# Four accumulator groups in every sum of a Runge-Kutta scan, and one matmul moved behind a signal

## The reference

```python
def _derivative(q, p, drive, coupling, bias):
    i_couple = jnp.tanh(q) @ coupling.T
    dq = q - q ** 3 / 3.0 - p + drive + i_couple + bias
    dp = EPSILON * (q + ALPHA - BETA * p)
    return (dq, dp)
# _rk4_step: dq1..dq4 at q, q + DT/2*dq1, q + DT/2*dq2, q + DT*dq3 (p likewise)
q_next = clip(q + DT / 6.0 * (dq1 + 2 * dq2 + 2 * dq3 + dq4), -CLAMP, CLAMP)
# FFN on the trace of q: gate_up = q_trace @ w_gu.T ; h = silu(gate) * up ; y = h @ w_down.T
# out = x + y / sqrt(mean(y * y) + EPS)
```

## Time and profile before

| | |
|---|---|
| median of 3 runs | 1477.7 us (1476.33 to 1479.62) |
| profiled execution | 1477.39 us, its span 1475.4 us |
| TensorE matmul busy | 1376.2 us, 93% |
| VectorE busy | 1393.8 us, 94%, 10250 instructions |
| ScalarE busy | 763.1 us, 52% |
| granted TensorE clock | 0.999 of full speed |

### The profile page before, as it was taken

One profiled execution on the slowest core, in us unless ns is written; L12 is line 12 of the kernel. 1 busy time (PEld: TensorE's weight loads), 2 busy tenths in 40 slices (PEclk: granted clock), 3 DMA queues, 4 the chain that ended last, 5 costly groups with the idle time before them and its releaser, 6 DMA issues. The chain is left out here.

```text
span 1475.4 us, 94031 instructions
## 1 busy us (share of the span) xinstructions
PE 1376.2 (93%) x38433; PEld 1266.5 (86%) x38433; DVE 1393.8 (94%) x10250; ACT 763.1 (52%) x5886; POOL 50.7 (3%) x89
## 2 busy tenths in 40 slices
PE   2567999999999999999999999999999999999998
PEld 0356899999999999989999999999999999998998
DVE  6999999999999999999999999999999999999991
ACT  4444555555555555555555555555555555555551
POOL 0441000000000000000000000000000000000000
PEclk9999999999999999999999999999999999999999
DMA  9200000010000000000000000001000000000000
GB/s 228 48 7 3 15 8 8 4 26 5 22 8 4 26 4 26 5 22 8 4 26 4 26 4 22 8 4 26 4 26 4 22 8 4 26 4 26 4 22 23
DMA packets 11955, 28.61 MB, mean 19 GB/s; under 512 B 1537, under 2 KB 5889, under 8 KB 11393
## 3 DMA queue, kind: packets, MB, share of 16 engines
q1 hardware_dynamic: 11520, 22.57, 6.0%
q10 hardware_dynamic: 2, 0.03, 0.0%
HBM read 18.40 MB, written 4.19 MB: 15 GB/s over the span
## 5 line engine op out<-in xcount | busy, mean ns | idle before, releaser
L634 PE MATMUL scan_ps<-th,wscan 128*128 128x32 f16 x32768 | 1000.5, 177 | 58.0 <-ACT th L674 35.7
L634 PEld LDWEIGHTS scan_ps<-th,wscan 128*128 128x128 f16 x32768 | 912.4, 96 | 153.6 <-ACT th L674 116.6
L674 ACT ACTIVATE th<-scan_ps 128x16 f16<-128x16 f32 x1536 | 275.1, 184 | 488.1 <-DVE scan_ps L780 488.1
L720 DVE TENSOR_TENSOR th<-t,th 128x16 f16<-128x16 f32 x2048 | 351.1, 174 | 31.3 <-ACT t L676 5.4
L367 PE MATMUL y_ps<-wffn,shared 128*128 128x128 f32 x1408 | 309.3, 303 | 0.0
L356 PE MATMUL gu_ps<-shared,raw 128*128 128x128 f16 x1408 | 286.3, 218 | 0.0
L676 ACT ACTIVATE t<-scan_ps 128x16 f32<-128x16 f32 x1536 | 268.6, 180 | 0.0
L356 PE MATMUL gu_ps<-shared,hi_early 128*128 128x128 f16 x1792 | 222.9, 218 | 0.2 <-DVE shared L383 0.2
L367 PEld LDWEIGHTS y_ps<-wffn,shared 128*128 128x128 f32 x1408 | 210.7, 190 | 0.0
L674 ACT ACTIVATE th<-q_raw 128x16 f16<-128x16 f32 x512 | 106.2, 207 | 170.1 <-DVE q_raw L780 161.3
L446 ACT ACTIVATE sum_r<-dr,constant 128x64 f32<-128x64 f32 x528 | 184.7, 352 | 17.5 <-DMA dr<-drive 17.5
(11 more groups left out here) (51 smaller groups left out, 1017.0 us busy)
## 6 DMA issues: line engine op xcount, KB each, us to landing
raw<-packed SPq DMA_DIRECT2D x11, 768.0 KB, 10.3
dr<-drive SPq DMA_DIRECT2D x34, 128.0 KB, 3.2
shared<-x SPq DMA_DIRECT2D x16, 256.0 KB, 3.7
out<-shared SPq DMA_DIRECT2D x16, 256.0 KB, 2.9
coup<-coupling_t SPq DMA_DIRECT2D x1, 1024.0 KB, 12.9
shared<-scales ACTq DMA_DIRECT2D x1, 33.0 KB
q_raw<-cond_t SPq DMA_DIRECT2D x1, 16.0 KB, 5.4
bias<-bias_t SPq DMA_DIRECT2D x1, 2.0 KB, 6.9
```

Of the source, the lines that this page charges most:

```text
L634: i = nc.tensor.matmul(to, wscan[:, w, part, kt, cols], moving, start=first, stop=last, skip_group_check=True)
L674: nc.scalar.activation(th[s % 2][:, c, 0, :], q, ACT.Tanh, scale=1.0 / S).then_inc(now.tanh_hi, 1)
L720: nc.vector.tensor_tensor(th[s % 2][:, c, 1, :], t32[:, c, :], th[s % 2][:, c, 0, :], ALU.subtract).then_inc(now.tanh_lo, 1)
```

## The change

- Every sum reads four groups (`four`). In stages 1 to 3 `cube` writes its result into `local_ps` and signals `first_half`; the linear part is written into `linear_ps` by `linear_second` (stage 1) or `linear_staged` (stages 2, 3) and signals as well. `local_in`, `q_cub`'s use, `with_q1[0]`, `with_q2[0]` and `with_q3`'s additions go, and so does `UNIT`.
- `with_p` is made row by row, four instructions of 128x32 with a factor each (`P_ROW`): row 0 and 2 in stage 0, rows 1 and 3 in stage 1. The setup's `with_p` goes.
- The last matmul of `couple(s,0,0,1)` is issued behind the one that signals `first_half`.
- The clip of `p_state` goes between the two sums of stage 3.
- `h32` and `norm_out` go to stages with s%4 = 3; by the schedule's arithmetic `norm_out` is in stages 19, 31 and 43 of a block in place of 26, 38 and 54. `make_x_lo` goes between the two low parts of stage 3.

```diff
-LOCALS = STEPS * 16
+LOCALS = STEPS * 13
...
-            ready[-1] += (2 - ready[-1]) % 4
+            ready[-1] += (3 - ready[-1]) % 4
...
-        free = [s for s in range(self.norm_sum + 3, 2 * STAGES) if s % 4 == 2 and s % STAGES not in taken]
+        free = [s for s in range(self.norm_sum + 3, 2 * STAGES) if s % 4 == 3 and s % STAGES not in taken]
...
-            def couple(s, part, k_half, n_half):
+            def couple(s, part, k_half, n_half, first_one=0, end=HC * HC):
...
+                        if not first_one <= c * HC + kt - k_half * HC < end:
+                            continue
...
                 couple(s, 0, 0, 0)
-                couple(s, 0, 0, 1)
+                couple(s, 0, 0, 1, 0, 3)
                 pe.wait_ge(now.tanh_lo, 2 * s + 2)
                 couple(s, 0, 1, 0).then_inc(now.first_half, 1)
+                couple(s, 0, 0, 1, 3)
                 couple(s, 1, 1, 1)
...
-                return local(nc.vector.scalar_tensor_tensor(halves(q_cub[:, :, :]), halves(q_sq[:, :, :]), OWN[i],
-                                                            q_stage[i - 1], ALU.subtract, ALU.mult))
-
-            def local_in(s):
+                nc.vector.scalar_tensor_tensor(local_ps, halves(q_sq[:, :, :]), OWN[i], q_stage[i - 1],
+                                               ALU.subtract, ALU.mult, reverse0=True).then_inc(now.first_half, 1)
+
+            def linear_second(q):
+                nc.vector.scalar_tensor_tensor(linear_ps.rearrange("p h (c b) -> p h c b", b=B),
+                                               quarters(q), float(BY[1, BY_Q1]), quarters(with_p[:, 1]),
+                                               ALU.mult, ALU.add).then_inc(now.first_half, 1)
+
+            def linear_staged(s, base):
                 i = s % 4
-                nc.vector.scalar_tensor_tensor(local_ps, halves(linear[i]), UNIT[i], halves(q_cub[:, :, :]),
-                                               ALU.mult, ALU.subtract).then_inc(now.first_half, 1)
...
+                nc.vector.scalar_tensor_tensor(linear_ps, q_stage[i - 2], float(BY[i, BY_Q1 + i - 1]),
+                                               halves(base[:, :, :]), ALU.mult, ALU.add).then_inc(now.first_half, 1)
+
+            def add_p(step, row):
+                return add(with_p[:, row], p_state[:, :, :], P_ROW[row], sum_r[:, step % STEPS, row])
...
+                dve.wait_ge(now.first_half, 3 * (s + 1))
+                nc.vector.tensor_reduce(q_half(following, 0), four[0], AX.X, ALU.add).then_inc(now.q_ready, 1)
+                if between:
+                    between()
                 dve.wait_ge(now.second_half, s + 1)
-                nc.vector.tensor_reduce(q_half(following, 1), slots[1], AX.X, ALU.add).then_inc(now.q_ready, 1)
+                nc.vector.tensor_reduce(q_half(following, 1), four[1], AX.X, ALU.add).then_inc(now.q_ready, 1)
```

More of the change, by code:

```diff
@@ L89 @@
 P_UNIT = BY_OWN[BY_Q4]
[L90 to L103, removed]
+P_ROW = [float(LINEAR[i, BY_P] * P_UNIT) for i in range(ROWS)]
+BY = LINEAR[:-1]
 P_SUM = [1.0, BY_OWN[BY_P] / (BY_OWN[BY_Q3] / P_UNIT), 1.0, BY_OWN[BY_Q3] / P_UNIT]
@@ L291, in program @@
         y_ps = [ctx.enter_context(nc.psum_tensor(f"y_ps{i}", [P, N], F32)) for i in range(2)]
-        prod, three, four = [], [], []
+        prod, four = [], []
         for half in range(2):
@@ L298, in program @@
             prod.append([both, high])
-            three.append(own[:, :, :, half:half + 3])
             four.append(own)
@@ L585, in _ @@
                 dve.wait_ge(sums_set, SUM_R_PARTS)
-                p_rows = p_state[:, :, :].unsqueeze(1).to_broadcast([P, ROWS, KT, B])
-                nc.vector.scalar_tensor_tensor(with_p[:, :], p_rows, P_ALL, sum_r[:, 0], ALU.mult, ALU.add)
         def q_half(i, half):
@@ L701, in dve_block @@
         def dve_block(dve, now, before, ffn, rest):
-            linear = [None, with_q1[0][:, :, :], with_q2[0][:, :, :], with_q3[:, :, :]]
             count = [0]
@@ L771, in ffn_part, with finish, next_p @@
                     dve_ffn(dve, *job)
[L773 to L780, removed]
-                dve.wait_ge(now.second_half, s + 1)
-                nc.vector.tensor_reduce(q_half(following, 1), slots[1], AX.X, ALU.add).then_inc(now.q_ready, 1)
+            def finish(s, between=None):
+                following = (s + 1) % 4
+                dve.wait_ge(now.first_half, 3 * (s + 1))
+                nc.vector.tensor_reduce(q_half(following, 0), four[0], AX.X, ALU.add).then_inc(now.q_ready, 1)
+                if between:
+                    between()
+                dve.wait_ge(now.second_half, s + 1)
+                nc.vector.tensor_reduce(q_half(following, 1), four[1], AX.X, ALU.add).then_inc(now.q_ready, 1)
+            def next_p(p4):
+                dve.wait_ge(now.local, p4)
+                local(nc.vector.tensor_scalar(p_state[:, :, :], p_part[3][:, :, :],
+                                              (-CLAMP - P_SHIFT) * S / P_UNIT, (CLAMP - P_SHIFT) * S / P_UNIT,
+                                              ALU.max, ALU.min))
             for t in range(STEPS):
@@ L797, in dve_block @@
                     dve.wait_ge(now.local, count[0])
-                rows = add_p(t, 0, 4)
+                row0 = add_p(t, 0)
                 if t == 1 and rest:
@@ L813, in dve_block @@
                     dve.wait_ge(before.clipped, STEPS)
-                dve.wait_ge(now.local, rows)
+                dve.wait_ge(now.local, row0)
                 linear_first(q1)
@@ L817, in dve_block @@
                 cube_first(q1, CLAMP * S if t or before else UNLIMITED)
-                add_q(with_q1[0], 1, BY_Q1, q1, with_p[:, 1])
-                add_q(with_q1[1], 2, BY_Q1, q1, with_p[:, 2])
+                add_p(t, 2)
                 finish(s)
                 s = 4 * t + 1
-                add(p_part[0][:, :, :], p_state[:, :, :], P_SUM[0], q1)
-                add_q(with_q1[2], 3, BY_Q1, q1, with_p[:, 3])
+                add_p(t, 1)
+                p1 = add(p_part[0][:, :, :], p_state[:, :, :], P_SUM[0], q1)
                 low_part(s, 0)
+                row3 = add_p(t, 3)
                 low_part(s, 1)
[L827 to L831, removed]
+                cube(s)
+                dve.wait_ge(now.local, p1)
+                linear_second(q1)
                 p2 = add_p_staged(1)
@@ L835, in dve_block @@
                 s = 4 * t + 2
+                dve.wait_ge(now.local, row3)
+                add_q(with_q1[1], 2, BY_Q1, q1, with_p[:, 2])
+                with_13 = add_q(with_q1[2], 3, BY_Q1, q1, with_p[:, 3])
+                low_part(s, 0)
+                low_part(s, 1)
+                cube(s)
+                dve.wait_ge(now.local, with_13)
+                linear_staged(s, with_q1[1])
+                with_23 = add_staged(with_q2[1], 3, BY_Q2, with_q1[2])
+                p3 = add_p_staged(2)
+                finish(s)
+                s = 4 * t + 3
                 ffn_part(s)
                 low_part(s, 0)
[L838 to L847, removed]
                 if t:
@@ L851, in dve_block @@
                     make_x_lo(dve, before, STEPS - 1)
-                low_part(s, 0)
                 low_part(s, 1)
-                cubed = cube(s)
+                cube(s)
                 dve.wait_ge(now.local, p3)
+                linear_staged(s, with_q2[1])
                 p4 = add_p_staged(3)
[L857 to L863, removed]
+                finish(s, lambda: next_p(p4))
             assert count[0] == LOCALS
```

3 lines of the change are left out of this document (removed).

## The result

The changed kernel takes 1482.18 us (1481.60 to 1482.52, 7 runs), the kernel before 1477.73 beside it (1476.33 to 1479.62, 7 runs): ratio 1.0024, 95% interval 1.0015 to 1.0034. It is slower, by 4.45 us in the medians. The profiled execution took 1482.52 us with a span of 1480.5, against 1477.39 and 1475.4 before: +5.1, and it is these 5.1 that the traces can be asked about. TensorE's mean granted clock is 0.999 of the full 2.4 GHz in both.

What follows compares the result with a forecast made beforehand. TensorE closes stages 2, 3, 0, VectorE stage 1, with a second-half loop of little slack. Loops +0.26 us per block, +4.1 over 16, plus norm_out's 3.3: +7.4 on 1477.39, 1484.7 us; 8-in-10 range 1474 to 1492.

Steps and rivals of the forecast that it cites:

- The moved matmul lengthens the second half's loop: Scan stages 1, 2, 3: second sum starts 0.225 us after the first, loop through the low part becomes 1.317.
- The wider sums alone: Six of eight sums per step go from 48 to 64 elements: +0.017 us per stage in stages 2, 3, 0.
- Stage 1 gains, VectorE is no longer late: Three issues behind the cube instead of five, VectorE ready some 0.2 us earlier; stage 1 falls from 1.375 to 1.317.
- norm_out in stage 3: Moved from stage 2, it puts 0.08 us on the path, 42 times: 3.3 us.
- Stage 0: It waits for its low part: 1.343 to 1.360 by the wider sum, 1.363 with next_p.
- Stages 1 to 3: The second half's loop through the low part closes these stages at 1.317 us, from 1.375, 1.288 and 1.296.
- the tanh alone (1): Second tanh binds, not the low part: stages 1 to 3 at 1.308, stage 0 at 1.359; 1478.3 us, chance 0.27.
- The first half's signal as the path (2): Second half has slack; stages 1 to 3 at 1.286, stage 0 at 1.335; 1460 us, chance 0.10.
- Busy time (3): VectorE's busy time is the bound: +61 ns per step, 15.6 us more, 1493 us, chance 0.06.
- VectorE late in stage 2 (4): New forms there or with next_p issue 0.03 us slower each: 7.7 us more, 1492 us, chance 0.09.

Runs made afterwards that it cites:

- the last experiment: Changed kernel with four matmuls ahead of the first half's signal, output in 4 parts of 128 columns, and VectorE's wait for the clearing later: 1473.87 us, ratio 0.9976.

## Why the prediction was right, and where its sizes were off

The forecast was 1484.7, the time is 1482.18, within the forecast's own range. Point by point:

1. *The moved matmul lengthens the second half's loop.* Right: second sum 0.226 behind the first (0.225 predicted), the 20th matmul straight behind the low part, stages 2 and 3 up to 1.321 and 1.322. Undone, the stages fall to the first half's loop and 8.0 us come back. The wider sums alone add 0.018 to 0.020 a stage (0.017).
2. *Stage 1 gains, VectorE is no longer late.* Right: 1.375 to 1.321 (1.317), its first sum 0.04 behind TensorE's 23rd matmul as in every other stage.
3. *norm_out in stage 3.* Right in place, somewhat too dear: 1.387, 1.379 and 1.383 at stages 19, 31 and 43 where I had 1.39, so 0.06 each instead of 0.08, 2.6 us instead of 3.3 (42 x 0.077 is 3.2). The reading of the cost before was off as well: 1.300 holds for stage 26 alone, stages 38 and 54 take 1.287 and 1.286, as without norm_out. A stage with it:
```profile
864.64 0.23 DVE L767 TENSOR_REDUCE scan_ps<-scan_ps 128x16 f32<-128x64 f32 x1
864.86 0.23 DVE L771 TENSOR_REDUCE scan_ps<-scan_ps 128x16 f32<-128x64 f32 x1
865.00 0.39 DVE L388 SCALAR_TENSOR_TENSOR shared<-y_ps,rinv,shared 128x176 f32<-128x176 f32 x1
865.31 0.17 DVE L704 TENSOR_TENSOR th<-t,th 128x16 f16<-128x16 f32 x1
865.39 0.19 DVE L398 SCALAR_TENSOR_TENSOR shared<-hist,shared 128x32 f16<-128x32 f32 x1
865.50 0.17 DVE L704 TENSOR_TENSOR th<-t,th 128x16 f16<-128x16 f32 x1
...
866.02 0.23 DVE L767 TENSOR_REDUCE q_raw<-scan_ps 128x16 f32<-128x64 f32 x1
```
Its second low part starts 0.86 behind the first sum, as worked out, against 0.79 in the plain stage from 830.83 above; of these 0.07 the stage shows 0.06.

4. *Stage 0*, mis-sized: 1.377 against 1.363 predicted, 12 x 16 x 0.014 = 2.7 us. ScalarE in stage 0, after (its two last rows) answers to two rows of before:
```profile
833.73 0.22 ACT L659 ACTIVATE th<-q_raw 128x16 f16<-128x16 f32 x1 [0.73 <-DVE q_raw L767]
833.85 0.20 ACT L661 ACTIVATE t<-q_raw 128x16 f32<-128x16 f32 x1
833.96 0.21 ACT L659 ACTIVATE th<-q_raw 128x16 f16<-128x16 f32 x1
834.08 0.20 ACT L661 ACTIVATE t<-q_raw 128x16 f32<-128x16 f32 x1
```
```profile
859.18 0.20 ACT L674 ACTIVATE th<-q_raw 128x16 f16<-128x16 f32 x1
859.29 0.20 ACT L676 ACTIVATE t<-q_raw 128x16 f32<-128x16 f32 x1
```
The second tanh and its fp32 copy, on which the low part waits, start 0.12 apart after and 0.11 (0.106 unrounded) before. Before, the second tanh came right behind the first pair; now that the second sum is later, it starts when that sum has ended, and its copy follows at the distance of the first pair, which starts from idle and stands 0.12 apart as well. I had kept the old distance. That a start from idle makes the distance is read from these rows and was not tried apart. In the medians the second tanh starts 0.017 later behind the first sum than before, its copy 0.031 and the end of the second low part 0.035: the difference of 0.014 between the first two is what the forecast lacked.

5. *Stages 1 to 3*, mis-sized by 0.004 to 0.005 each: 40 x 16 x 0.004 = 2.6 us too little. From the second sum to the end of the second low part the medians of stage 3 give 0.716 before and 0.735 after: 0.019 for the wider sum where I had 0.017.
6. *What the forecast left out*, both in the other direction: block 0 (-3.55 us), where VectorE's two-SBUF-input additions stand against POOL; and the three stalls of stage 60 (-2.3 us), which I had seen as "POOLq L893 1.3" in the earlier trace rows and had said of POOL's clearing only that it has room.

So in blocks 1 to 15, without the stalls, the loops lost 11.1 us where I had 7.4 (over 16 blocks); 3.55 + 2.3 + 0.13 were given back; 5.1 is left. The forecast stood close partly because errors of both signs cancelled.

The rivals: the tanh alone (1) would leave stages 1 to 3 at 1.308, they are at 1.321. The first half's signal as the path (2) fell, undoing it is faster. Busy time (3) fell: its working added up durations and expected 15.6 us more, the page counts overlapping ones once and has 30 us less busy, and the kernel takes 4.45 us more. The Trainium skill, "Perfetto Trace Analysis", section "Identifying the Most-Contended Engine", takes VectorE's occupancy as a fair measure of how near it is to its limit; read as what the time follows, it would have had a faster kernel here, and the runs go against that reading. VectorE late in stage 2 (4) fell: its sum follows TensorE by 0.04 there too.

## What to carry to other kernels

In a loop over several engines, signal a first half early only if the second half has more slack than what is moved behind it; measure that slack from the end of the second half's last input to the next release, in the stage where the wait is seen. In this kernel an instruction's length counted where it stands between two waits of the loop, whatever its engine's busy share. Beside the steady loop look at the first block, and at the rare row with a large wait: here these two moved the total by more than the forecast's error.

## What was not expected of the hardware

- VectorE's 128x32 operations with two SBUF inputs that start 0.05 to 0.27 us into a POOL operation of 0.67 take 0.46 to 0.68 (those that start 0.03 before its end keep their 0.19), against 0.20 without; making POOL's operations small takes 9.9 us off block 0 of the kernel before.
- Clearing the semaphores on POOL takes 0.16 us, but it stands 6.5 to 8.2 us in the wait behind the last output part in the kernel before, for the store and the load after it, and VectorE starts 0.03 behind the end of the clearing. The spread of the kernel before, 4.7 us in one set of 19 runs, goes down to 0.6 in 11 runs with the wait moved; whether the stalls are what spreads it I did not test.
- In the last experiment the stage in which a second wait stands ahead of the sum is 0.07 us longer in every block, with no wait of VectorE for POOL in its trace. The trace puts it at the wait instruction ahead of the sum (0.065 from its start to the sum's); the wait was not tried apart there.
- TensorE's granted clock fell to 1.2 GHz for 3.4 us behind four of the stalls of the run with late output parts, 2.5 us in all.
